# Attention scores in 64-row groups, key blocks written masked from PSUM, and the maxima's rows moved by DMA

## The reference, cut to what matters

```
h = layernorm(x); qkv = h @ w_qkv.T          # 16 heads of 8 features
take the tokens in snake order; cut into 4 segments of 128 queries
keys and values of a segment: every second token (64)
scores = (q * 8**-0.5) . k ; attn = softmax(scores) ; o = attn @ v
x = x + layernorm(o @ w_out.T)
h = layernorm(x)
x = x + layernorm(sum over the top 2 of 8 experts + sigmoid gate * shared expert)
```

## Time and profile before

| | us |
|---|---|
| median of three runs (181.62, 181.83, 206.29) | 181.83 |
| the profiled execution's own time | 178.82 |
| its span | 177.0 |
| mean granted TensorE clock, share of full speed | 0.97 |
| TensorE busy | 152.5 |
| VectorE busy | 135.0 |
| ScalarE busy | 114.0 |
| GpSimd busy | 49.5 |

### The profile page before, as it was taken

One profiled execution on the slowest core, in us unless ns is written; L12 is line 12 of the kernel. 1 busy time (PEld: TensorE's weight loads), 2 busy tenths in 40 slices (PEclk: granted clock), 3 DMA queues, 4 the chain that ended last, 5 costly groups with the idle time before them and its releaser, 6 DMA issues.

```text
span 177.0 us, 3700 instructions
## 1 busy us (share of the span) xinstructions
PE 152.5 (86%) x1214; PEld 130.2 (74%) x1214; DVE 135.0 (76%) x505; ACT 114.0 (64%) x270; POOL 49.5 (28%) x51
## 2 busy tenths in 40 slices
PE   6889798896699963999789999999999899999910
PEld 5678676684489851899478887979997899979910
DVE  7788899338956899368958876958999945996792
ACT  3769576753976567464496669944779376757703
POOL 5621100422000470002200220259652089301221
PEclk9999999999799999699999999999999999999995
DMA  5991550000000000000000000000000200010101
GB/s 172 286 321 56 119 124 0 2 4 0 0 4 0 0 4 0 0 0 6 0 2 4 0 0 4 0 0 6 0 0 2 63 0 2 12 47 4 59 0 59
DMA packets 10625, 6.01 MB, mean 34 GB/s; under 512 B 752, under 2 KB 10608, under 8 KB 10608
## 3 DMA queue, kind: packets, MB, share of 16 engines
q1 hardware_dynamic: 10192, 5.58, 11.2%
q10 hardware_dynamic: 416, 0.21, 0.4%
HBM read 3.69 MB, written 1.05 MB: 27 GB/s over the span
## 4 chain that ended last, share of the span: by engine, by line
PE 64%; DVE 24%; ACT 4%; issue 4%; POOL 1%; POOLq 0%; ACTq 0%; DVEq 0%
PE bank L694 15%; PE bank L499 7%; PE bank L360 6%; DVE negm L1241 5%; PE bank L362 5%; PE bank L361 5%; PE bank L357 4%; PE bank L476 3%; DVE Kb L1218 3%; PE bank L516 3%; DVE ST L1131 2%; PE bank L549 2%; DVE X L1403 2%; DVE NM L1187 2%; PE bank L535 1%
## 5 line engine op out<-in xcount | busy, mean ns | idle before, releaser
L304 POOL TENSOR_TENSOR RS<-VE,nhalf 128x4 f32<-128x4 f32 x14 | 14.1, 1010 | 83.4 <-DVE VE L1139 83.4
L1403 DVE SCALAR_TENSOR_TENSOR X<-bank,CW,X 128x128 f32<-128x128 f32 x80 | 22.5, 343 | 7.8 <-PE bank L694 7.7
L694 PEld LDWEIGHTS bank<-w2n,Pr 128*128 128x128 f32 x192 | 25.0, 191 | 2.0
L1241 DVE TENSOR_REDUCE negm<-bank 128x8 f32<-128x512 f32 x32 | 20.7, 684 | 7.3 <-PE bank L476 7.2
L694 PE MATMUL bank<-w2n,Pr 128*128 128x128 f32 x192 | 25.2, 275 | 0.0
L910 ACT ACTIVATE Pr<-bank 128x512 f32<-128x512 f32 x32 | 17.8, 598 | 10.9 <-PE bank L499 10.9
L1034 ACT ACTIVATE Pr<-bank 128x512 f32<-128x512 f32 x27 | 16.3, 605 | 11.9 <-PE bank L362 11.8
L499 PE MATMUL bank<-Qs,Kb 128*128 128x128 f32 x128 | 18.1, 280 | 0.4 <-ACT Qs L850 0.2
L499 PEld LDWEIGHTS bank<-Qs,Kb 128*128 128x128 f32 x128 | 16.7, 196 | 1.9 <-issue 0.7
L360 PE MATMUL bank<-XH,w1h 128*128 128x512 f32 x32 | 15.1, 473 | 0.0
L320 POOL TENSOR_TENSOR Tm<-Tm 128x512 f32<-128x512 f32 x7 | 9.0, 1291 | 20.4 <-ACT Tm L1049 20.4
(11 more groups left out here) (165 smaller groups left out, 378.8 us busy)
## 6 DMA issues: line engine op xcount, KB each, us to landing
X<-in_L_attn_x SPq DMA_DIRECT2D x4, 256.0 KB, 4.0
Kb<-kone SPq DMA_DIRECT2D x8, 128.0 KB, 2.4
XP<-in_x_snake SPq DMA_DIRECT2D x3, 256.0 KB, 3.6
out<-XN SPq DMA_DIRECT2D x3, 256.0 KB, 2.2
w1n<-in_L_ffn_w SPq DMA_DIRECT2D x1, 512.0 KB, 5.1
w2n<-in_L_ffn_w SPq DMA_DIRECT2D x1, 512.0 KB, 6.2
out<-XN SPq DMA_DIRECT2D x2, 128.0 KB, 1.8
wqkv_n<-in_L_attn_w_qkv SPq DMA_DIRECT2D x1, 192.0 KB, 3.0
```

Of the source, the lines that this page charges most:

```text
L694: i = mm(ps[output_bank(n, s)][:, s * P:(s + 1) * P], lhs[:, s * P:(s + 1) * P], w, start=True, stop=True)
L1241: V.tensor_reduce(negm[:, b % 2, s, 8 * half:8 * half + 8], bank(S1[n % 2], 8, KEYS), AX.X, ALU.max, negate=True).then_inc(S["mx"], 1)
L1403: V.scalar_tensor_tensor(out=acc[:, b, t], in0=ps[output_bank(n)][:, t * P:(t + 1) * P], scalar=CW[:, b, t, k:k + 1], in1=acc[:, b, t], op ...
```

## The change

1. **Rows.** A group now lies in four quadrants of 32 rows, one head in each: 8 rows high, 8 high again (for the low keys), 8 low, and 2 rows for the maximum's two parts. `head_order` permutes the columns of w_qkv for this. `sel` becomes 1544 columns; every select matmul has 128 stationary columns in place of 96.
2. **Both scores contract 64 rows.** Rows 0 to 63 (row group r = 0) and 64 to 127 (r = 1) are multiplied apart, with 128 stationary and 128 moving columns, eight matmuls a tile in `scores_q` and eight in `scores_k`. r = 0 writes one bank and r = 1 the other, in turn; so both banks must be free at the start. In `scores_k_part`, used for batch 3, four matmuls of one row group follow one another.
3. **Key blocks.** `Kb` holds two masked versions in place of four; ScalarE writes groups 0 and 1 straight from PSUM (for batch 0 the second pair of tiles), VectorE groups 2 and 3, with a scale and a bias for each row; the bias writes the ones for the maxima. `Ks`, `kone` and its eight DMAs go.
4. **Maxima's rows.** ScalarE copies the transposed maxima once to `mrows`; two DMAs on SP's queue spread them over the quadrants of `Qs`. The second copy of ScalarE and VectorE's copy go. For batch 0 the two stand in SP's queue between the loads of w1 and w2.
5. **Order.** For batch 0 `x_T(1)`, `qkv(1)` and `qk_low(1)` come later; `max_T(0)` comes before `select_k(1)`; `scores_k(i,0)` comes after `scores_q(i+1,0)`; for batch 3 the parts (1,0) and (1,1) are adjacent. One of batch 0's `q_rows` goes to VectorE, the clearing of `Mq` to GpSimd.

```diff
+            def max_rows(b):
+                sp.wait_ge(S["mev"], b + 1)
+                for j in range(2):
+                    sp.dma_start(Qs[MROW + j:P:32, b % 2].bitcast(F32),
+                                 mrows[H * j:H * (j + 1)].bitcast(F32)).then_inc(S["mdma"], 16)
+            max_rows(0)
...
-            sp.wait_ge(S["kones"], 1)
-            for u in range(2):
-                for s in range(NT):
-                    sp.dma_start(Kb[MROW:P, u, :, s].bitcast(F32), kone[MROW:P].bitcast(F32)).then_inc(kdma[u], 16)
+            for b in range(1, B):
+                max_rows(b)
...
+            nc.gpsimd.memset(Mq[:].bitcast(F32), 0.0).then_inc(S["mzero"], 1)
...
+            def scores_q(b, s):
+                m = b * NT + s
...
+                if m >= 1:
+                    pe.wait_ge(S["mx"], 2 * m)
+                for g in range(G):
...
+                    for r in range(2):
+                        rows = slice(PART * r, PART * (r + 1))
+                        i = mm(S1[r][:, g * P:(g + 1) * P], Qs[rows, b % 2, g, s * P:(s + 1) * P],
+                               Kb[rows, b % 2, g, s], start=True, stop=True)
+                        if g == G - 1:
+                            i.then_inc(S["s1"], 1)
...
+            def key_scores(b, s, g, r):
+                rows = slice(PART * r, PART * (r + 1))
+                return mm(S2[s2_bank((b * NT + s) * 2 + r)][:, g * P:(g + 1) * P], Kb[rows, b % 2, g, s],
+                          Qs[rows, b % 2, g, s * P:(s + 1) * P], start=True, stop=True)
+            def scores_k(b, s):
+                m = b * NT + s
+                if s == 0:
+                    pe.wait_ge(S["mdma"], 32 * (b + 1))
+                if m >= 1:
+                    pe.wait_ge(S["ex"], 2 * m)
+                for g in range(G):
+                    for r in range(2):
+                        i = key_scores(b, s, g, r)
+                        if g == G - 1:
+                            i.then_inc(S["s2"], 1)
+            def scores_k_part(b, s, r):
+                if s == 0 and r == 0:
+                    pe.wait_ge(S["mdma"], 32 * (b + 1))
+                pe.wait_ge(S["ex"], (b * NT + s) * 2 + r)
+                for g in range(G):
+                    i = key_scores(b, s, g, r)
+                i.then_inc(S["s2"], 1)
...
             scores_q(0, 0)
             select_q_0(1, 0)
             select_q_0(1, 1)
-            x_T(1)
             values(0)
             scores_q(0, 1)
+            warm_up(2, TH, PC)
+            scores_q(0, 2)
+            x_T(1)
             warm_up(1, TH, PC)
-            scores_q(0, 2)
+            scores_q(0, 3)
             qkv(1)
-            scores_q(0, 3)
+            max_T(0)
             select_k(1)
-            warm_up(2, TH, PC)
...
                 select_q(i + 1, 3)
-                if i >= 1:
-                    scores_k(i, 0)
                 scores_q(i + 1, 0)
+                scores_k(i, 0)
                 if i >= 1:
                     project(i - 1)
                 scores_k(i, 1)
...
-            scores_k(i, 0, (0,))
             up(0)
             project(i - 1)
-            scores_k(i, 0, (1,))
+            scores_k_part(i, 0, 0)
             expert_h(0, 0)
-            scores_k(i, 1, (0,))
+            scores_k_part(i, 0, 1)
             shared_o(0)
-            scores_k(i, 1, (1,))
+            scores_k_part(i, 1, 0)
+            scores_k_part(i, 1, 1)
...
+            def key_blocks(b):                                   # ScalarE
+                act.wait_ge(S["ks_ps"], 2 * b + 1)
...
+                for a in range(2):
+                    A(Kb[:, b % 2, 0:2, :, a], PA[:].rearrange("p (g s k) -> p g s k", g=2, k=KEYS), ACT.Identity,
+                      scale=cst[:, C_KM + a:C_KM + a + 1], bias=cst[:, C_KO + a:C_KO + a + 1]).then_inc(S["kb_a"], 1)
...
+            def key_blocks(b):                                   # VectorE
+                dve.wait_ge(S["ks_ps"], 2 * b + 2)
...
+                for a in range(2):
+                    V.tensor_scalar(Kb[:, b % 2, 2:4, :, a], PBk[:].rearrange("p (g s k) -> p g s k", g=2, k=KEYS),
+                                    cst[:, C_KM + a:C_KM + a + 1], cst[:, C_KO + a:C_KO + a + 1],
+                                    ALU.mult, ALU.add).then_inc(S["kb_d"], 1)
...
             def max_rows(b):                                     # ScalarE
                 act.wait_ge(S["mT_ps"], b + 1)
-                if b >= 2:
-                    act.wait_ge(S["s2"], 8 * (b - 1))
-                for g in range(2):
-                    A(Qs[MROW:P, b % 2, g], PC[MROW:P, 0:T], ACT.Copy).then_inc(S["mev_a"], 1)
+                if b >= 1:
+                    act.wait_ge(S["mdma"], 32 * b)
+                A(mrows[:], PC[0:2 * H, 0:T], ACT.Copy).then_inc(S["mev"], 1)
```

More of the change, by code:

```diff
@@ L42 @@
 TANH = 4
-MROW = 96
+Q4 = P // 32
+MROW = 3 * HD
+PART = P // 2
 C_ID = 0
-C_HM = C_ID + P
-C_ONE = C_HM + HG
-C_VM = C_ONE + G * HG
+C_KM = C_ID + P
+C_KO = C_KM + 2
+C_VM = C_KO + 2
 C_IO = C_VM + 2
 C_END = C_IO + E
+SEL_Q = 0
+SEL_K = SEL_Q + 4 * P
+SEL_L = SEL_K + 4 * P
+SEL_END = SEL_L + 4 * P + HD
 def hidden_bank(n):
@@ L192, in program @@
         ld_x0 = [sem(f"ld_x0_{h}") for h in range(2)]
-        kdma = [sem(f"kdma{u}") for u in range(2)]
         ident = cst[:, C_ID:C_ID + P]
@@ L486, in max_T @@
                 i.then_inc(S["mT_ps"], 1)
-            def scores_k(b, s, halves=(0, 1)):
-                for half in halves:
-                    n = (b * NT + s) * 2 + half
-                    pe.wait_ge(*((S["mev_d"], b + 1) if half else (S["mev_a"], 2 * b + 2)))
-                    if b < 2 and s == 0 and half == 0:
-                        pe.wait_ge(kdma[b], 16 * NT)
-                    if n >= 2:
-                        pe.wait_ge(S["ex"], n if b == B - 1 else n - 1)
-                    for j in range(4):
-                        g, pr = 2 * half + j // 2, j % 2
-                        i = mm(S2[s2_bank(n)][:, j * P:(j + 1) * P],
-                               Kb[:, b % 2, g, s, 2 * pr:2 * pr + 2],
-                               Qs[:, b % 2, g, s * P:(s + 1) * P], start=True, stop=True)
-                    i.then_inc(S["s2"], 1)
+            def key_scores(b, s, g, r):
[20 more added lines that the diff above has]
+                i.then_inc(S["s2"], 1)
             def attend(b, s):
                 if s == 0:
-                    pe.wait_ge(S["mev_a"], 2 * b + 2)
+                    pe.wait_ge(S["mev"], b + 1)
                 if NT * b + s >= 1:
@@ L962, in _ @@
             qk_high(1)
-            k_rows(1, 0)
-            k_rows(1, 1)
+            max_rows(0)
+            key_blocks(1)
             for i in range(B - 1):
                 p1 = i + 2 < B
-                if i == 0:
+                q_rows(i + 1, 0)
+                if i >= 1:
                     max_rows(i)
-                    q_rows(i + 1, 0)
-                    q_rows(i + 1, 1)
-                    exps(i, 0)
-                    q_rows(i + 1, 2)
-                else:
-                    q_rows(i + 1, 0)
-                    max_rows(i)
-                    for g in range(1, G - 1):
-                        q_rows(i + 1, g)
+                q_rows(i + 1, 1)
+                q_rows(i + 1, 2)
+                if i >= 1:
                     o_copy(i - 1)
-                    exps(i, 0)
+                exps(i, 0)
+                if i >= 1:
                     y_copy(i - 1)
@@ L1533, in constants @@
     p = np.arange(P)
-    for h in range(HG):
-        c[:MROW, C_HM + h] = (p[:MROW] % 32) // HD == h
-    for h in range(H):
-        c[MROW:, C_ONE + h] = (p[MROW:] - MROW) % H == h
+    for a in range(2):
+        mine = p // 32 % 2 == a
+        c[:, C_KM + a] = mine
+        c[:, C_KO + a] = mine & (p % 32 // 2 == MROW // 2)
     for j in range(2):
```

217 lines of the change are left out of this document (101 added, 116 removed), and 4 rows, old and new, of the table names.

## The result

The changed kernel takes 199.28 us, the median of four runs (194.07, 195.78, 202.77, 204.02), and the kernel before 181.73 us on the same chip. The recorded ratio is 1.0861, with a 95% interval of 1.0705 to 1.1017; it and the ratios of the experiments leave out executions that are marked as disturbed (the two longest here), and the quotient of the medians of all runs is 1.097. The predicted 184.3 us was wrong, and so was the range up to 191. The profiled execution took 195.78 us with a span of 194.0, against 178.82 and 177.0 before.

What follows compares the result with a forecast made beforehand. TensorE was taken as nearly full from 90 us on, in turns with VectorE and ScalarE from 53 to 77. Prologue +2.0, key blocks -1.35 twice, DMA +1.35, +0.1, -0.2, batch 3 +1.9: +2.5 on 181.83, 184.3 us; range 177.5 to 191.

Steps and rivals of the forecast that it cites:

- Second rival: Score matmuls: row groups don't run side by side, eight steps, 0.89 us a call; +6.5 on the forecast, 190.8 us; chance 0.2.
- the overlap: Score calls on TensorE: two row groups run side by side, so eight matmuls take four steps of 0.11, 0.44 us.
- Key blocks: VectorE before the division: two 512-element instructions, 1.38 us against 2.73, 1.35 us less on the path; ScalarE's copies taken as equal.
- The prologue: Batch 0 and i = 0: the new order delays qkv(1) and later work; attend(0,0) near 31.5 instead of 29.52, +2.0 us.
- The DMA at i = 1: Maxima's rows: ScalarE's copy comes late, two DMAs take about 2.7 us, scores_k(1,0) waits; the key blocks' 1.35 gain is eaten.
- The wait that the prediction named as its test: Before scores_k(1,0) at i = 1: TensorE waits for the maxima's DMA; the prediction fails if this wait is missing.
- the +1.35: Sum's DMA term at i = 1: the maxima's DMA costs 1.35 us, cancelling the key blocks' gain there.
- third rival: Maxima's DMA costs 3.7 us instead of 2.7 and shows at i = 1, i = 2 and batch 3: +3, 187 us; chance 0.15.
- The other signs of this stage: Stage i = 1: output_T(0) near 49.2 us and attend(1,0) near 55.3 us.
- i = 2: Third turn: key blocks take 1.35 off, the DMA hides, +0.1 for q_rows; attend(2,0) near 77.8 us.
- Batch 3: Its attention among expert products: switches some 1.3 us, adjacent parts' stall 0.8, DMA 0.1, less 0.3; sum +1.9 us.
- First rival: Relief of VectorE and ScalarE decides, new order costs nothing, the half clock goes: about -4, 178 us; chance 0.25.

Runs made afterwards that it cites:

- e3: Changed kernel with nine dummy 256-column matmuls at each of TensorE's two waits in the loop's first turn: 200.55 us, ratio 1.098.
- e2: Kernel before, both scores contracting only rows 0 to 63, the other rows left out: 205.4 us against 181.99.
- e4: Changed kernel, with all four score matmuls of one row group issued before the other group's four: 195.13 us, ratio 1.081.
- e7: Kernel before, with only rows 0 to 63 in the second (key) scores of batch 3: 192.32 us, ratio 1.052.
- e1: Changed kernel with all 128 rows contracted in every matmul of both scores: 192.97 us, ratio 1.064.
- e5: Changed kernel with all 128 rows in batch 3's key scores alone: 188.56 us, ratio 1.024.
- e6: Changed kernel with 128 rows in both scores and four dummy 256-column matmuls at each of two first-turn waits: 194.02 us, ratio 1.059.
- e8: Kernel before with dummy 128-column matmuls in the wait before output_T, four at i = 1 and eight at i = 2: 179.32 us, ratio 0.979.
- e12: Kernel before with e11's dummy matmuls plus seven more around select_k(i + 2) for i = 0 and 1: 178.97 us against 184.04.
- e10: Changed kernel with all 128 rows in the key scores of all batches, 64 rows kept in scores_q: 189.69 us against 184.04.
- e9: Kernel before with scores_q in eight matmuls of 128 moving columns a tile instead of four of 256, same 96 rows: 187.0 us against 184.04.
- e11: Same program as e8 (kernel before, dummy matmuls before output_T), run again in more rounds: 179.32 us against 184.04.

## Why the prediction was wrong, step by step

**The step that failed is TensorE's clock.** The prediction gave the half clock no term in the sum. It let pieces of it "come or go at 1 us each" in the forecast's own range, and otherwise priced every matmul at full clock. The trace has 51.2 us at half clock ahead of the last `attend` where there were 6.8. In batch 3, where the path is TensorE all through, 17.1 us at half clock come with 8.2 us more, of which the parts' longer steps explain 0.6 (below); the steps of 0.59 and 1.04 us at either clock make the rest. In the second segment e3 puts the clock at 3.6 of 4.4 us.

**Its cause, as far as it is shown.** Score matmuls that contract 64 rows in place of 96 or 128 go with stretches of many us at half clock, with TensorE busy all the time. For batch 3 this is shown: from (3,0) to (3,3) the five profiles with 64 rows there (changed, e2, e3, e4, e7) take 16.6 to 19.8 us with 11.3 to 19.1 us at half clock, and the nine with whole rows (before, e1, e5, e6 and e8 to e12) 10.5 or 10.6 us at full clock. e2 and e7 make it in the kernel before, e5, e10 and e1 unmake it in the changed kernel. Whether the missing rows count or the switches to the tiled array that come with them is not separated, and the router products inside batch 3 are in all of these profiles. For the other stretches the rows are not the whole cause: e1 has a stretch of 17.1 us at half clock, and e6 two of 20.5 and 10.2, without any 64-row matmul. No row that I had showed it: in the earlier trace rows the clock falls behind 2.26 us of idle time. A rule of the Trainium skill, "TensorE: Matmul & The Clock Gate" (Part 1), ties the clock to how busy the array has been; by busy time the window from 108 to 126 us, 18.00 of 18 us, should have had full clock, and was granted 0.53. The measurement decides: being busy was not enough here.

**The first stretch has a second cause.** It begins at 33 us behind two new waits of the first turn (TensorE's timeline of the changed kernel):

```profile
26.67 0.50 PE L475 MATMUL bank<-qch,sel 128*128 128x512 f32 x1 [1.07 <-ACT Kb L926]
...
32.11 0.66 PE L526 MATMUL bank<-Qs,Kb 64*128 64x128 f32 x8 [1.17 <-ACT Pr L955]
```

e1 has them and falls without any 64-row matmul, and e3, which fills them, doesn't fall there. Why the clock stays down for 17 to 24 us then, and for 3.4 in the kernel before, is open: neither short moving operands (e9) nor the waits alone (e6) give it.

**Second rival and the overlap.** TensorE's timeline of the changed kernel, a dense tile at full clock, and one call at half clock:

```profile
64.05 0.66 PE L526 MATMUL bank<-Qs,Kb 64*128 64x128 f32 x8
64.64 0.44 PE L576 MATMUL bank<-cst,AVs 128*128 128x128 f32 x2
65.00 0.65 PE L563 MATMUL bank<-Pr,Vb 128*32 128x128 f32 x16
65.58 0.66 PE L510 MATMUL bank<-Kb,Qs 64*128 64x128 f32 x8
...
43.96 1.12 PE L526 MATMUL bank<-Qs,Kb 64*128 64x128 f32 x8
45.01 0.69 PE L576 MATMUL bank<-cst,AVs 128*128 128x128 f32 x2
```

Eight take 0.59 us from start to next start, the forecast's 0.44 and one switch of 0.12, where e1 needs 0.93. So the row groups run side by side, as the Trainium skill's "TensorEngine Tiling (Array Packing)" (Key Properties) says of tiles, and the second rival's mechanism is refuted, though the time went past its 190.8 us. At half clock the call costs 1.05, more than the whole-array call of the earlier trace rows at full clock.

**Key blocks.** VectorE's and ScalarE's, of batches 2 and 1, in their timelines of the changed kernel, and VectorE's division behind them:

```profile
51.90 1.52 DVE L1265 TENSOR_SCALAR Kb<-bank,cst 128x512 fp32r<-128x512 f32 x2
53.34 0.35 DVE L1297 RECIPROCAL rden<-bank 128x32 f32<-128x32 f32 x1
...
25.17 1.45 ACT L926 ACTIVATE Kb<-bank,cst 128x512 fp32r<-128x512 f32 x2 [0.49 <-PE bank L465]
```

VectorE: 1.44 us up to the division, against 2.73 in the earlier trace rows; forecast 1.38, right. ScalarE: 1.45 us for two, 0.73 each, where I had two of 0.60; missed by a quarter us. It ends at 26.62, 1.1 later than the 25.5 that I gave, and TensorE waited for it for 1.07.

**The prologue.** `attend(0,0)` at 32.70, forecast 31.5: the direction right, the size +3.2 in place of +2.0. `scores_k(0,0)` starts at 30.32 us, 0.6 behind the forecast's 29.7, behind the first of the two waits above; the rest is in the second, for both exponentials, which I had named and priced at two exponentials of 0.5 us, where the earlier trace rows has 0.60, and their latencies.

**The DMA at i = 1.** Timelines of the changed kernel, of SP's queue, VectorE and TensorE, and below it TensorE's of e1:

```profile
55.44 1.11 SPq L264 DMA_DIRECT2D Qs<-mrows  x2
...
57.65 0.69 DVE L1274 CAST Qs<-bank 128x512 fp32r<-128x512 f32 x1 [3.50 <-PE bank L476]
...
58.39 0.33 PE L510 MATMUL bank<-Kb,Qs 64*128 64x128 f32 x2 [0.32 <-DVE Qs L1274]
58.56 0.61 PE L526 MATMUL bank<-Qs,Kb 64*128 64x128 f32 x8
```

```profile
62.78 1.11 PE L526 MATMUL bank<-Qs,Kb 128*128 128x128 f32 x8 [0.32 <-DMA Qs<-mrows]
```

The wait that the prediction named as its test is missing in the changed kernel: `scores_k(1,0)` starts at 58.56 with no idle time before it, 3.1 us after SP turned to the first DMA, and what came in last was VectorE's `q_rows`. In e1, which is at full clock there, the wait exists. SP turns to the two at 59.92 and the matmul starts at 62.78: a way of 2.9 us, for which I had 2.7, but only 0.32 us of it show (0.44 in e10). So the way was right, its cover was mis-sized, and of the +1.35 some 0.3 to 0.4 is left; the third rival with its 3.7 us is refuted, since SP takes 1.11 us for the two issues and not 1.66. The other signs of this stage failed, mostly by the clock: `output_T(0)` at 55.09 us for 49.2, `attend(1,0)` at 60.93 for 55.3. What ate the key blocks' gain was the clock: the chain of waits of the changed kernel has each pair of `select_q` at 0.86 us in this piece, and at 0.56 just behind it.

```profile
54.44 0.43 PE bank L475
54.86 0.43 PE bank L476
...
57.00 0.32 PE bank L475
57.32 0.24 PE bank L476
```

**i = 2.** From `attend(1,0)` to `attend(2,0)` the changed kernel takes 22.7 us against 23.7, with the same half clock in both, 3.4 us. It is the one segment where the clock falls out of the comparison, and it gives -1.0 for a forecast of -1.2 (77.8 less 55.3, against 23.7). The relief of VectorE is real.

**Batch 3.** The adjacent parts cost a stall, 0.69 us at 105.27 for 0.8 forecast. A part of four takes 0.59 us at full clock, 0.15 more than four steps of 0.11: eight parts make 1.2 us, for 1.3 forecast. Both lie in the fourth segment as much as in the fifth. There is no term of the prediction for the rest of +8.2, some 7.6 us; that is clock, since e5 has 10.5 us there.

**First rival.** Its gain on VectorE was there, but not the end of the half clock that it counted on: that grew. What is left of +17.3 once the clock is set aside is +3.2, about +0.8 (e3), -1.0, about +0.6 in batch 3 and, in the fourth segment, a part of +2.5 (6.8 us of it were at half clock), which no run separates. That makes +3.6 or somewhat more, against the forecast's +2.5; the forecast failed by the clock all the same.

## What to carry to other kernels

Price a change to TensorE's work twice, by its steps and by the clock that the stretch around it will be granted: here two row groups did eight score matmuls in 0.59 us in place of 0.93, and in batch 3 the 64 rows went with 11 to 19 us of dense work at half speed. When a page shows 5s in its row of the granted clock, take the steps of one group at either level before looking for any other cause. Where TensorE waits for another engine, a few cheap matmuls in the wait can be worth more than they cost (e8, e11), but not where they outlast it (e3), and not surely where they fit (e6).

## What was unexpected of the hardware

- Matmuls that contract 64 rows go with half clock in windows with little or no idle time: 0.62 with TensorE busy 18.00 of 18 us (e7), 0.51 with 33.44 of 35 (e2).
- The clock also falls with whole rows and no idle time just ahead: 0.51 from 98 to 108 us behind 7.00 us of 7 (e6).
- Two row groups run side by side even when one's four matmuls are issued ahead of the other's four: 0.60 us for eight (e4).
- Stretches at half clock last from 3.4 us (before) to 34.1 us (e2).
- Executions of one kernel differ by their granted clock: the kernel before took 179.2 us at 0.960 and 190.4 at 0.908.
- Dummy matmuls in a wait of TensorE made the kernel before faster by 2.1% [0.7, 3.5] (e8).
